# Attention's inverse transform in two mirrored halves, and the moments of x on ScalarE

## The reference

```
x = x + autocorrelation(layernorm(x), ctx, ctx)       # stage 1
x = x + lora_ffn(layernorm(x))                        # stage 2
x = x + channel_attention(layernorm(x), ctx)          # stage 3: top 154 of 256 times of each ctx channel
x = x + experts(layernorm(x))                         # stage 4

def autocorrelation(Q, K, V):                         # per channel, along time, L = 256
    corr = ifft(fft(q) * conj(fft(k))).real
    w, idx = top_k(corr, 11);  w = softmax(w)
    out[pos] = sum_i w[i] * v[min(idx[i] + pos, L - 1)]
```

## Time and profile before

| | |
|---|---|
| Time, median of 3 runs | 3469.47 us (3467.81 to 3471.97) |
| The profiled execution | 3478.11 us, span 3476.5 us |
| TensorE busy | 3210.4 us, 92% of the span |
| VectorE busy | 2716.1 us, 78% |
| ScalarE busy | 2041.5 us, 59% |
| GpSimd busy | 1652.8 us, 48% |
| Attention stage | about 0 to 1390 us |
| Mean granted TensorE clock | 0.956 of 2.4 GHz |

### The profile page before, as it was taken

The page is one execution under the profiler, slowest core; times in us unless marked ns, Lnnn a source line. Parts: engine busy times, 40 slices in busy tenths (PEclk is TensorE's granted clock), DMA queues, the critical chain, the costliest instruction groups (busy, mean ns, idle before and its releaser), DMA issues. The chain is left out here.

```text
span 3476.5 us, 50587 instructions
## 1 busy us (share of the span) xinstructions
PE 3210.4 (92%) x12866; PEld 1737.5 (50%) x12866; DVE 2716.1 (78%) x7121; ACT 2041.5 (59%) x5464; POOL 1652.8 (48%) x1164
## 2 busy tenths in 40 slices
PE   4999999999999997899999999999999999368897
PEld 2666666666666665444444444444444444222332
DVE  4888888888888886676877879687878879567775
ACT  4565555555565652665675757566675856465561
POOL 5989898889888985001212121121212120034565
PEclk9999999999999999999999999999999999588887
DMA  5554444544444433354554746354464735524552
GB/s 169 159 153 144 135 135 140 154 137 134 135 150 144 137 111 118 113 158 134 171 154 133 201 127 192 110 166 165 154 165 134 209 124 133 151 94 187 212 205 97
DMA packets 264661, 516.61 MB, mean 149 GB/s; under 512 B 33286, under 2 KB 133385, under 8 KB 241433
## 3 DMA queue, kind: packets, MB, share of 16 engines
q1 hardware_dynamic: 235164, 406.92, 38.0%
q10 hardware_dynamic: 18240, 71.34, 7.0%
q0 software_dynamic: 11008, 35.66, 3.0%
HBM read 384.81 MB, written 129.04 MB: 148 GB/s over the span
## 5 line engine op out<-in xcount | busy, mean ns | idle before, releaser
L957 PE MATMUL acc<-xh,wq 128*128 128x512 f16 x4096 | 1212.0, 383 | 52.1 <-DVE xr L1611 19.8
L957 PE MATMUL acc<-xl,wq 128*128 128x512 f16 x2048 | 761.4, 381 | 0.0
L1182 ACT ACTIVATE unused<-c_first,minus_guess 128x256 bf16<-128x256 f32 x1024 | 505.2, 494 | 298.5 <-DVE minus_guess L1485 231.4
L957 PEld LDWEIGHTS acc<-xh,wq 128*128 128x128 f16 x4096 | 400.2, 99 | 543.8 <-issue 44.8
L886 POOL DMA_DIRECT2D c_first<-ctx_pairs x120 | 66.5, 554 | 881.1 <-DVE mk L1536 866.6
L419 PE MATMUL bu<-m_iz,zf 128*128 128x256 f32 x2048 | 457.5, 382 | 9.2 <-POOL zf L261 9.2
L419 PEld LDWEIGHTS bu<-m_iz,zf 128*128 128x128 f32 x2048 | 393.0, 192 | 92.3 <-issue 41.5
L957 PEld LDWEIGHTS acc<-xl,wq 128*128 128x128 f16 x2048 | 201.3, 98 | 245.7 <-issue 6.6
L438 PE MATMUL bx<-m_ic,pf 128*128 128x256 f32 x1024 | 238.5, 387 | 6.8 <-POOL pf L261 6.8
L438 PEld LDWEIGHTS bx<-m_ic,pf 128*128 128x128 f32 x1024 | 191.9, 192 | 33.5 <-POOL pf L261 7.7
L554 DVE TENSOR_TENSOR prod_e<-by,kf 128x1024 f32<-128x1024 f32 x64 | 78.4, 1225 | 156.6 <-PE by L386 156.6
(11 more groups left out here) (328 smaller groups left out, 6963.6 us busy)
## 6 DMA issues: line engine op xcount, KB each, us to landing
wq<-w_split SPq DMA_DIRECT2D x512, 256.0 KB, 3.0
x_first<-x SPq DMA_DIRECT2D x16, 2048.0 KB, 7.6
c_first<-ctx SPq DMA_DIRECT2D x64, 512.0 KB, 7.0
xt<-xT SPq DMA_DIRECT2D x64, 512.0 KB
x_pairs<-xo SPq DMA_DIRECT2D x64, 512.0 KB, 3.2
c_first<-ctx_pairs POOLq DMA_DIRECT2D x128, 256.0 KB, 4.4
x<-xn_pairs SPq DMA_DIRECT2D x32, 1024.0 KB, 6.5
out_pairs<-ost SPq DMA_DIRECT2D x32, 1024.0 KB, 4.7
```

Of the source, the lines that this page charges most:

```text
L957: return pe.matmul(acc[b][:], ws[(WQ * o + k // CK) % WR][:, k % CK, a, :], x[:, k, :], start=start, stop=False)
L1182: act.activation(signs[:, u // 2, t] if n == COUNTS - 1 else unused[u % 2][:], ct[k % CR][:, t], ACT.Sign, bias=guess[q % 2][:, u:u + 1], ...
```

## The change

Four things change together.

The basis of the inverse transform, m_iz, is laid out by mirrored times. The output columns stand for the times 255 down to 129 (columns 0 to 126) and 0 to 128 (columns 127 to 255), see time_of_column. Cosine terms are the same at mirrored times and sine terms opposite, so each of the four parts is multiplied into one half of the columns only (MIRROR): 129, 127, 128 and 128 columns instead of 256 each. One term, that of the highest frequency, sits in the sine part's first row but is even; it gets a matmul of its own with one partition.

The halves are joined by a butterfly: ScalarE copies the half with columns 0 to 126 of all four tiles out of PSUM into xo, and VectorE writes the difference and the sum back into bu, waiting once between the two.

All that meets x1 in this layout is reordered in the arrays that come in and go out: xT, ctx_pairs, out_pairs. The exact phase gets ctx_in_time, and the sampled times and MOVES of ffn_phase change; its instructions don't.

The moments of x move from VectorE to ScalarE. Per batch: two passes over 2048 columns with an accumulator (mean, in steps k % 4 = 1 and 2), the negated means, and eight squares of 512 columns with an accumulator (squares, in steps k % 4 = 2 and 3). VectorE keeps one small tensor_reduce (variance). The tile ident is allocated and filled outside the stage's own list of tiles, with the same load.

```diff
+    iz = np.zeros((4, F, L))
+    iz[0, :, F - 1:] = 2 * np.cos(even.T * ahead)
+    iz[0, 0, F - 1:] = 1.0
+    iz[1, 1:, :F - 1] = -2 * np.sin(even.T * back)[1:]
+    iz[1, 0, F - 1:] = alt(ahead)
+    iz[2, :, :F - 1], iz[2, :, F - 1] = 2 * np.cos(odd.T * back), 2.0
+    iz[3, :, F:] = -2 * np.sin(odd.T * ahead)[:, 1:]
...
+    PIECES = 4
+    MIRROR = ((P - 1, L), (0, P - 1), (0, P), (P, L))
...
                             for a in range(a0, a0 + TT):
-                                mm = pe.matmul(bu[:, j // 2, (j % 2) * L:(j % 2 + 1) * L], zf[s][:, a, j * P:(j + 1) * P], m_iz[:, a, :], start=a == 0 and j % 2 == 0, stop=a == 2 * TT - 1 and j % 2 == 1)
+                                c0, c1 = MIRROR[a]
+                                mm = pe.matmul(bu[:, j // 2, (j % 2) * L + c0:(j % 2) * L + c1], zf[s][:, a, j * P:(j + 1) * P], m_iz[:, a, c0:c1], start=a == 0 and j % 2 == 0, stop=a == 2 * TT - 1 and j % 2 == 1)
+                            if a0 == 0:
+                                c0, c1 = MIRROR[0]
+                                pe.matmul(bu[:, j // 2, (j % 2) * L + c0:(j % 2) * L + c1], zf[s][0:1, 1, j * P:(j + 1) * P], m_iz[0:1, 1, c0:c1], start=False, stop=False)
...
+            def mean(it, k, a):
...
+                act.activation(xn[slot][:, a, :], xn[slot][:, a, :], ACT.Copy, accum_out=total[:, a:a + 1]).then_inc(ln_sum, 1)
+                if a == TT - 1:
...
+                    act.activation(negative[:], total[:], ACT.Copy, scale=-1.0 / D).then_inc(ln_mean, 1)
...
+            def squares(it, k, a):
...
+                for n in range(PIECES):
+                    at = TT * PIECES * b + PIECES * a + n
+                    if n or a or least(b, 1):
+                        act.wait_ge(ln_sq, at)
+                    act.activation(unread[:], xn[slot][:, a, n * D // PIECES:(n + 1) * D // PIECES], ACT.Square, bias=negative[:, a:a + 1], accum_out=parts[:, a, n:n + 1]).then_inc(ln_sq, 1)
...
                 split_step(it, k)
+                mean(it, k, 1)
+                squares(it, k, 1)
                 if f is not None:
...
+                if g is not None:
...
+                    act.wait_ge(i_mm, g + 1)
...
+                    act.activation(xo[s][:, :, 0:P - 1], bu[:].rearrange("p b (h t) -> p (b h) t", h=2)[:, :, 0:P - 1], ACT.Copy).then_inc(odd_sb, 1)
+                mean(it, k, 0)
+                squares(it, k, 0)
                 if t is not None:
                     act.wait_ge(t_mm, t + 1)
...
-                moments(it, k, 1, (0, 1, 2))
-                moments(it, k, 2, (3, 4, 5))
-                moments(it, k, 3, (6, 7))
+                variance(it, k)
                 if g is not None:
...
-                    dve.wait_ge(i_mm, g + 1)
+                    whole = bu[:].rearrange("p b (h t) -> p (b h) t", h=2)
+                    minus, plus = whole[:, :, 0:P - 1], whole[:, :, P:L - 1]
+                    odd = xo[s][:, :, 0:P - 1]
+                    dve.wait_ge(odd_sb, g + 1)
+                    dve.tensor_tensor(minus, plus, odd, ALU.subtract).then_inc(apart_ok, 1)
+                    dve.wait_ge(apart_ok, g + 1)
+                    dve.tensor_tensor(plus, plus, odd, ALU.add).then_inc(joined_ok, 1)
+                    dve.wait_ge(joined_ok, g + 1)
...
-    MOVES = (1.0, 0.9, 0.7, 0.5)
+    MOVES = (1.0, 0.8, 0.5, 0.35)
```

More of the change, by code:

```diff
@@ L116, in attention_phase @@
         wcol = sb("w_cols_sb", [P, LAST])
-        st = [sb(f"st{i}", [P, TT, NST, 6]) for i in range(2)]
-        mv = sb("mv", [P, TT, 2])
+        unread = sb("unread_squares", [P, D // PIECES], BF16)
+        total, negative = sb("x_total", [P, TT]), sb("minus_mean", [P, TT])
+        parts, var = sb("var_parts", [P, TT, PIECES]), sb("var", [P, TT])
         std = sb("std", [P, TT])
@@ L533, in step @@
                 if b is not None:
[L534 to L535 removed]
+                    act.wait_ge(ln_mv, b + 1)
+                    act.activation(std[:], var[:], ACT.Sqrt, bias=eps[:], scale=1.0 / D).then_inc(ln_std, 1)
                 if g is not None:
@@ L555, in products, with variance @@
                 dve.tensor_tensor(out[:, 2:4, :], src, spectrum[:, 1:3, :], ALU.mult).then_inc(mul, 1)
-            def moments(it, k, r, pieces):
-                b = batch(it, k - r)
+            def variance(it, k):
+                b = batch(it, k - 3)
                 if b is None:
                     return
-                slot = ((k - r) // CH) % 2
-                if r == 1:
-                    dve.wait_ge(x_in[slot], 16 * (it + (k - r) // STEPS + 1))
-                for n in pieces:
-                    dve.bn_stats(st[slot][:, n // NST, n % NST, :], xn[slot][:, n // NST, n % NST * 512:(n % NST + 1) * 512]).then_inc(ln_bn, 1)
-                if r < 3:
-                    return
-                n_ready, n_used = counted(dve, TT * NST * (b + 1)), counted(dve, TT * b)
-                dve.wait_ge(consts_in, 16 * N_CONST)
-                dve.wait_ge(ln_bn, n_ready)
+                dve.wait_ge(ln_sq, TT * PIECES * (b + 1))
                 if least(b, 1):
-                    dve.wait_ge(consts_in, 16 * N_CONST)
-                    dve.wait_ge(ln_scale, n_used)
-                for a in range(TT):
-                    dve.bn_aggr(mv[:, a, :], st[slot][:, a, :, :]).then_inc(ln_mv, 1)
+                    dve.wait_ge(ln_std, b)
+                dve.tensor_reduce(var[:], parts[:], AX.X, ALU.add).then_inc(ln_mv, 1)
             def scales(it, k):
@@ L1711, in ffn_phase, with exact_masks_phase @@
     return again
-def exact_masks_phase(nc, ctxT, xn3, masks, feat, again, keep):
-    NPAIR, _, KT, T = ctxT.shape
+def exact_masks_phase(nc, ctx_in_time, xn3, masks, feat, again, keep):
+    NPAIR, _, KT, T = ctx_in_time.shape
     L = T // 2
@@ L1723, in exact_masks_phase @@
     FEATURES = 6
+    H = L // 2
+    MARKS = L - H
     stack = ExitStack()
@@ L1794, in _ @@
                     dve.wait_ge(stored, 16 * at)
-                    for b in range(2):
-                        t = slice(b * L, (b + 1) * L)
-                        dve.tensor_scalar(m[:, t], left[:, t], NEG, None, ALU.is_le).then_inc(mask_ok, 1)
+                    m2, left2 = m[:].rearrange("p (b t) -> p b t", b=2), left[:].rearrange("p (b t) -> p b t", b=2)
+                    dve.tensor_scalar(m2[:, :, H - 1:L], left2[:, :, 0:H + 1], NEG, None, ALU.is_le).then_inc(mask_ok, 1)
+                    for c2 in range(H - 1):
+                        dve.tensor_scalar(m2[:, :, c2:c2 + 1], left2[:, :, L - 1 - c2:L - c2], NEG, None, ALU.is_le).then_inc(mask_ok, 1)
                     x2 = x[:].rearrange("p (b t) -> p b t", b=2)
-                    dve.wait_ge(mask_ok, 2 * at + 2)
+                    dve.wait_ge(mask_ok, MARKS * at + MARKS)
                     dve.wait_ge(x_in, 16 * at + 16)
@@ L2392, in layouts @@
     segments = D // (2 * P)
+    order = time_of_column(L)
+    to_pairs = lambda v: v.reshape(NB // 2, 2, L, D // P, P).transpose(0, 4, 3, 1, 2).reshape(NB // 2, P, D // P, 2 * L)
     neighbours = np.zeros((P, 2, P), np.float32)
@@ L2425 @@
     out = r.results[0]["out_pairs"].reshape(NB // 2, P, D // P, 2, L)
-    return np.ascontiguousarray(out.transpose(0, 3, 4, 2, 1).reshape(NB, L, D))
+    in_columns = out.transpose(0, 3, 4, 2, 1).reshape(NB, L, D)
+    return np.ascontiguousarray(in_columns[:, np.argsort(time_of_column(L))])
```

60 lines of the change are left out of this document (39 added, 21 removed).

## The result

The changed kernel takes 3507.65 us (median of 4 runs, 3498.93 to 3514.04), the kernel before 3469.91 in the same session (4 runs): the ratio is 1.0107, 95% interval 1.0082 to 1.0132. It is slower by 1.1%, about 38 us, and the sign and the range of the prediction held. The reason that it gave for the larger part of the loss did not: TensorE's clock never fell in a steady step, that is, in a step outside the start, the tail and the loop's jumps.

A forecast was written before the change was run, and what follows sets the result against it. VectorE was taken to bound three steps in four, a circle through VectorE and TensorE the others. 3478.1 + 9.5 - 8.5 + 0.5 - 3 + 28 = 3504.6 us profiled, 3496 as median after 8.6 off; range 3458 to 3530.

The forecast's parts named there:

- neither circle: Attention steps: VectorE's own loop (20.24 us) and one through TensorE (19.88 us) decide; the inverse transform is in neither.
- bu at 4.4 us: Inverse transform on TensorE: claimed to take 4.4 us in place of 7.1, opening a 2.4 us pause.
- 40 x 0.111: Inverse transform: 40 instructions priced at 0.111 us each, the rate of float32 instructions of 128 columns.
- Clock falls +28: 62 attention steps: pauses before the transposes lower TensorE's clock in some steps, costing 28 us in all.
- three in ten: Attention steps: assumed share of pauses followed by a clock fall, each costing about 1.5 us.
- a fall in nearly every step: Rival for the attention steps: the clock falls nearly every step, +84 us, total 3552; chance 0.08.
- Before's own two falls, -3: Attention stage: two clock falls already in the kernel before, counted inside the new falls, so 3 us subtracted.
- 57 steps -8.5: Attention steps in the repeating pattern of four: -0.6 us per four steps, -8.5 us over 57.
- with 1.1 us left: ScalarE: the w_back copy behind four squares was to finish 1.1 us before VectorE wants it, costing nothing.
- Start +9.5: Start of the attention stage: moments on ScalarE delay the first normalization and second batch, +9.5 us, ends 4 and 13.
- Five steps at the end: Last attention steps, without moments: each loses 0.1 us, +0.5 us in all.
- No falls: Rival: TensorE's clock stays at 1.00 throughout the attention stage, the same sum without 28, 3468 us; chance 0.20.

The follow-up runs named there:

- e4: The kernel before, with 128 of 256 columns in each inverse-transform instruction and nothing in place of the other half; 3575.70 us.
- e1: The changed kernel with the added one-partition matmul run on all 128 partitions, same values; 3512.65 us.
- e7: The changed kernel reordered on each engine to use the halves, with the added matmul on all partitions and the first batch's moments on VectorE; 3436.93 us.
- e8: The reordered version of e7 with the attention loop written out in full; 3409.61 us.
- e6: The changed kernel with the attention loop written out in full, no instruction on data differing; 3488.07 us.
- e12: The changed kernel once more, unchanged, for a second trace; 3502.75 us.

## Why the prediction was right, and where it was wrong

- **Bounds of the step: right.** bu is in neither circle (e4's unfallen steps), the transposes wait for wk, VectorE's circle decides with 2.08 us of waiting.
- **bu at 4.4 us: wrong, and the rest hangs on it.** The step that failed is "40 x 0.111": the earlier trace rows priced instructions on 128 partitions, and 8 of the 40 run on one. They take 0.21 and slow the next ones to 0.16; bu took 6.1 us, of which e1 gives 1.5 back. TensorE's pause was 0.7 us, and 1.1 in one step of four, not 2.4, and TensorE was busy 94% of 600 to 1100 us, not 85%.
- **Clock falls +28: measured 0.** The term was sized for a pause that the kernel does not have. Where the pause is nearly that long (2.2 to 2.7 us, e1) there are 0.27 falls a step at 0.9 to 1.6 us, close to the forecast. That closeness is partly luck: a recount of the trace before finds 14 pauses of 2.2 to 2.9 us with 7 low stretches, not 11 with 5, and three in ten was chosen below the count without a row. The rival of a fall in nearly every step is out for this pause length, since 45 of e1's 62 steps kept the clock. The Trainium skill's TensorE: Matmul & The Clock Gate, Part 4, from which it came, is not refuted by that. After, with at most 1.1 us of pause and 1.0 of transposes, cannot test it, and e7 and e8 speak for it: the clock fell there in steps whose longest pause is 1.8 us, with the 1.1 us of transposes between the two pauses. No run replaces the transposes by other work, so it stays open.
- **Before's own two falls, -3: measured 0.** They belong to the jumps (24 and 48), and after has three there (16, 24 and 32).
- **57 steps -8.5: measured +7.4.** 3.4 of it are the jumps, which the prediction did not see as a cost that can vary. The others are +0.35 in four steps where -0.6 stood. The largest part, 0.6, is the step with four squares: w_back, counted as hidden "with 1.1 us left", comes so late that w_fold starts 3.74 us behind wrec (e6 shows that it decides there whether xo stands at 1.53 or 1.80), since a square behind another takes up to 0.85 us in place of 0.74. Some 0.2 is xo at 1.80 in place of 1.56 in the step that had no moments, and 0.1 the step with the new reduction, which gained nothing.
- **Start +9.5: right** (8.1, and 9.5 in e12's trace).
- **The tail: the term that was missing.** "Five steps at the end" were priced, not the last two inverse transforms, which nothing hides: +8.5. All of it goes with the one-partition matmuls and the clock that stays low beside them, since e1, with the copy and the two additions still there, has 48.7 us where before has 48.8, its shorter bu paying for them.
- **Total.** The sum gave 3504.6 for an execution like the profiled one, and 3498.9 came, because the wrong +28 stood in for the tail (8.5) and for what the 57 steps missed (7.4 + 8.5). The medians lie 17 us further apart than the profiled executions, which no term had. So the range held by luck in its largest term. "No falls" was the true case of the list, and the prediction's own sign for it, a clock of 1.00 in the stage, appeared (600 to 1100 us); its sum of 3468 was wrong because it left out the tail and had the steady steps and the jumps 16 us too low.

## What to carry to other kernels

A shorter instruction stream on the busiest engine is worth nothing while the engine waits inside a circle that does not contain it; find the circle, change the order so that the work comes into it, and only then shorten. Price each instruction by a row of its own shape, partitions included. Price a software pipeline's first and last steps by themselves: there each added microsecond is paid in full.

## What the hardware showed

- Float32 matmul instructions of 129 columns whose weights and data lie on one partition take 0.21 us where those on 128 take 0.11, and the next four are slowed to 0.16 (after against e1). At the low clock it is 0.36, and 0.29 for the next four, where all take 0.21 in e1. The Trainium skill (TensorE: Matmul & The Clock Gate, Step-by-step: what each phase is for) says that the number of rows does not matter to a weight load. The trace agrees for the load (0.18 us on one row, 0.19 on 128); load and product together are what takes longer, of which that sentence says nothing.
- From step 62 to the FFN, where TensorE has little else to do, the clock was low for 36 to 45 us in the five traces with one-partition matmuls and for 12 to 25 in the nine without; after and e1, which differ in that alone, have 45 and 23.
- Taking work from TensorE made the kernel 102 us slower (e4), by a pause of 3.1 us a step after which the clock fell from 2.4 to 1.2 GHz in nearly every step.
- A jump back to a loop's start costs VectorE 2 to 4.6 us, with what follows some 17 to 23 us in this stage over five jumps; a step of the loop takes up to 0.27 us more than the same step written out.
